# Two expert stages with short TensorE loop bodies, the bias added tile by tile, and 496 unrolled scatters

## The reference

```
h = gelu(einsum('td,edh->teh', xf, W1) + b1)      # 256 -> 512, every expert on every node
y = einsum('teh,ehd->ted', h, W2) + b2            # 512 -> 256
out = einsum('ted,te->td', y, gate)               # 8 experts, gate 0 or 1; then 4 experts, soft gate
```

## Time and profile before

| | |
|---|---|
| Median of three runs | 4744.22 us |
| Profiled execution, span | 5102.1 us |
| First expert stage, first POOL copy to first DVE instruction of the next stage | 1688.0 to 2725.6 us |
| PE in that stage, start of first and last matmul | 1694.2 and 2450.2 us |
| Second expert stage, the same of PE | 4718.8 and 5085.9 us |
| Busy: PE / DVE / ACT / POOL | 2674 / 1894 / 1149 / 2164 us |

### The profile page before, as it was taken

One profiled execution on the slowest core, in us unless ns is written; L12 is line 12 of the kernel. 1 busy time (PEld: TensorE's weight loads), 2 busy tenths in 40 slices (PEclk: granted clock), 3 DMA queues, 4 the chain that ended last, 5 costly groups with the idle time before them and its releaser, 6 DMA issues. The chain is left out here.

```text
span 5102.1 us, 58668 instructions
## 1 busy us (share of the span) xinstructions
PE 2674.1 (52%) x11127; PEld 1856.8 (36%) x11128; DVE 1893.5 (37%) x4714; ACT 1149.0 (23%) x3778; POOL 2164.1 (42%) x2734
## 2 busy tenths in 40 slices
PE   3223945665542399999203777774100001635898
PEld 2123923333321277777102333333100000423676
DVE  5600265656557711111002222223444445465411
ACT  0010022222210111111001111111466666310111
POOL 0165045555530665565562666660466665000000
PEclk8555556666655699999656666665555555555999
DMA  2111422222220000000001333330000000000000
GB/s 71 40 41 60 181 55 76 79 78 76 72 59 0 25 10 17 9 20 1 1 1 41 90 88 88 90 90 17 5 5 5 5 5 4 0 0 11 19 9 25
DMA packets 118123, 199.51 MB, mean 39 GB/s; under 512 B 54417, under 2 KB 81158, under 8 KB 115910
## 3 DMA queue, kind: packets, MB, share of 16 engines
q0 software_dynamic: 75360, 124.95, 10.1%
q1 hardware_dynamic: 42726, 74.12, 4.2%
HBM read 186.58 MB, written 12.36 MB: 39 GB/s over the span
## 5 line engine op out<-in xcount | busy, mean ns | idle before, releaser
L493 POOL DMA_INDIRECT a0rows<-table,a0idx x462 | 469.6, 1016 | 517.6 <-ACT a0idx L478 403.8
L493 POOL DMA_INDIRECT a1rows<-table,a1idx x444 | 421.5, 949 | 325.3 <-ACT a1idx L478 175.5
L950 POOL DMA_INDIRECT erecords<-sc_slot x416 | 408.5, 982 | 328.3 <-POOL sc_slot L946 311.7
L523 PE MATMUL a1ps<-a1rows,a1w 128*128 128x256 f32 x888 | 428.1, 605 | 191.9 <-DMA a1rows<-table,a1idx 135.3
L523 PE MATMUL a0ps<-a0rows,a0w 128*128 128x257 f32 x924 | 416.3, 585 | 177.0 <-DMA a0rows<-table,a0idx 82.7
L1146 POOL DMA_INDIRECT gt_land<-table_gat,gt_idx x324 | 356.8, 1101 | 249.9 <-POOL gt_idx L1141 162.2
L1341 ACT ACTIVATE gt_parts<-gt_nb,gt_land 128x128 f32 x1296 | 414.8, 392 | 20.7 <-DVE gt_parts L1191 1.8
L1363 PE MATMUL gt_psT<-k_ident,gt_top 128*128 128x128 f32 x100 | 27.9, 434 | 702.2 <-DVEq L1196 702.2
L749 PE MATMUL f0dn<-f0w,f0hid 128*128 128x256 f32 x1600 | 353.3, 380 | 61.9 <-DVE k_x L797 61.9
L523 PEld LDWEIGHTS a1ps<-a1rows,a1w 128*128 128x128 f32 x888 | 212.0, 279 | 408.1 <-issue 283.5
L764 PE MATMUL f0up<-k_xnT,f0w 128*128 128x320 f32 x1280 | 352.9, 435 | 12.8 <-DMA f0b<-in_f_b 12.8
(11 more groups left out here) (366 smaller groups left out, 4185.1 us busy)
## 6 DMA issues: line engine op xcount, KB each, us to landing
es_ea<-in_eaT SPq DMA_DIRECT2D x16, 1664.0 KB
es_lane<-lane_row SPq DMA_DIRECT2D x16, 832.0 KB
f0w<-in_f_W SPq DMA_DIRECT2D x16, 512.0 KB
a0rows<-table,a0idx POOLq DMA_INDIRECT x462
a1rows<-table,a1idx POOLq DMA_INDIRECT x444
erecords<-sc_slot POOLq DMA_INDIRECT x416
table<-k_tbl SPq DMA_DIRECT2D x10, 650.0 KB, 3.5
gt_land<-table_gat,gt_idx POOLq DMA_INDIRECT x324
```

The lines of the kernel that those rows point to most:

```text
L493: pool.indirect_dma_start(rows[:, i, 0:TW], None, table, bass.IndirectOffsetOnAxis(ap=idx[:, i:i + 1], axis=0)).then_inc(gathered[i], 16)
L523: nc.tensor.matmul(sum_of(t), w[:, i, :], rows[:, i, 0:width], start=False, stop=False).then_inc(agg_done, 1)
L950: pool.indirect_dma_start(self.rec_dram, bass.IndirectOffsetOnAxis(ap=slot[:, i, 0:1], axis=0), slot[:, i, 1:R + 1], None).then_inc(self.p ...
```

## The change

It has three parts, all in the functions around `emit_experts`, and nothing else of the kernel is touched.

1. **PE, ACT and DVE loops.** PE has an outer loop over expert pairs and in it two inner loops of 5 trips, one for each weight buffer. A trip is a step. The 640 columns of a step are now worked as 3 tiles and 2 tiles: 4 slices of 384 columns, then 4 slices of 256, then 3 down tiles and 2 down tiles. The outer loop is opened with an option that places its head at slot 0 of an instruction page. The up results use 2 PSUM banks of one slice each, the down results 5 banks, one per tile of a group. A down tile waits for the addition of the same tile in the step before. ACT has the same two-level loop and 8 Gelu instructions per step, of 384 and 256 columns, instead of 4 of 640.
2. **Bias.** DVE adds the bias for the 5 tiles of one step (L720 of the changed kernel), drains, and then adds the 5 down results of that step (L725).
3. **Scatters.** `DirectScatter` replaces `Scatter` for `sb` and `sc`: 496 indirect DMAs written out one after another with constant addresses, which read their records and their destination rows from the columns of `recg` and `rece` themselves. There is no copy, no wait on a copy and no register arithmetic. From the ninth on each waits for the transfer eight before it.

```diff
-    STEPS, HALF = 2 * OUT, U * P // 2
+    PER = 2 * KH
+    HALVES = ((0, 3), (3, U))
-        hid = [sb(f"hid{i}", [P, KH, 2, HALF], F32) for i in range(2)]
+        hid = [sb(f"hid{i}", [P, KH, (b - a) * P], F32) for i, (a, b) in enumerate(HALVES)]
-        up = [ctx.enter_context(nc.psum_tensor(f"{tag}up{i}", [P, 2, 512], F32)) for i in range(2)]
-        down = [ctx.enter_context(nc.psum_tensor(f"{tag}dn{i}", [P, 512], F32)) for i in range(4)]
+        up = [ctx.enter_context(nc.psum_tensor(f"{tag}up{i}", [P, 512], F32)) for i in range(2)]
+        down = [ctx.enter_context(nc.psum_tensor(f"{tag}dn{i}", [P, 512], F32)) for i in range(U)]
+        def add_tiles(v, e, g):
+            x_of = lambda j: S.x[:, bass.ds(g * (U * D) + j * D, D)]
+            gate_of = lambda j: gate[:, bass.ds(g * U + j, 1), bass.ds(e, 1)].rearrange("p a b -> p (a b)")
+            for j in range(U):
+                nc.vector.scalar_tensor_tensor(x_of(j), b2_rows[:, bass.ds(e, 1), :].rearrange("p a d -> p (a d)"), gate_of(j),
+                                               x_of(j), ALU.mult, ALU.add)
+            v.drain()
+            for j in range(U):
+                v.wait_ge(down_done, U + (e * OUT + g) * U + j + 1)
+                nc.vector.scalar_tensor_tensor(x_of(j), down[j][:, 0:D], gate_of(j), x_of(j), ALU.mult, ALU.add).then_inc(added, 1)
+            v.drain()
...
         def _(pe):
-            pe.sem_inc(down_done, 1)
-            with pe.Fori(0, n_experts // 2) as o:
-                def down_step(s):
...
-                for s in range(STEPS):
...
+            pe.sem_inc(down_done, U)
+            with nc.Fori(0, n_experts // 2, engines=[pe.engine], head_slot={pe.engine: 0}) as o:
+                for i in range(2):
+                    with pe.Fori(0, OUT) as g:
+                        turn = o * (2 * OUT) + (g + i * OUT)
+                        pe.wait_ge(arrived[i], o * 48 + 48)
+                        for half, (a, b) in enumerate(HALVES):
+                            size = (b - a) * P
+                            for m in range(KH):
+                                q = half * KH + m
+                                pe.wait_ge(hid_ready, turn * PER + q + 1)
+                                for k in range(KD):
+                                    ins = nc.tensor.matmul(up[q % 2][:, 0:size], w1[i][:, k, m * P:(m + 1) * P],
+                                                           S.xnT[:, k, bass.ds(g * (U * P) + a * P, size)],
+                                                           start=(k == 0), stop=(k == KD - 1))
+                                ins.then_inc(up_done, 1)
+                        for half, (a, b) in enumerate(HALVES):
+                            pe.wait_ge(hid_ready, turn * PER + (half + 1) * KH + 2)
+                            for j in range(a, b):
+                                pe.wait_ge(added, turn * U + j + 1)
+                                for k in range(KH):
+                                    ins = nc.tensor.matmul(down[j][:, 0:D], hid[half][:, k, (j - a) * P:(j - a + 1) * P],
+                                                           w2[i][:, k, :], start=(k == 0), stop=(k == KH - 1))
+                                ins.then_inc(down_done, 1)
...
         def _(v):
-            with v.Fori(0, n_experts) as e:
-                for t in range(NT):
-                    nc.vector.scalar_tensor_tensor(S.x[:, t * D:(t + 1) * D], b2_rows[:, bass.ds(e, 1), :].rearrange("p a d -> p (a d)"),
-                                                   gate[:, t, bass.ds(e, 1)], S.x[:, t * D:(t + 1) * D], ALU.mult, ALU.add)
-                v.drain()
...
+                with v.Fori(0, OUT) as g:
+                    add_tiles(v, e, g)
...
+class DirectScatter:
...
+    def run(self, pool):
+
+        R = self.rec.shape[2]
+        for c in range(self.first, self.last):
+            turn, lane = divmod(c - self.first, 8)
+            if turn:
+                pool.wait_ge(self.put[lane], 16 * turn)
+            pool.indirect_dma_start(self.rec_dram, bass.IndirectOffsetOnAxis(ap=self.rec[:, c + 1, 0:1], axis=0),
+                                    self.rec[:, c + 1, 1:R], None).then_inc(self.put[lane], 16)
...
-            beside = (Scatter(nc, S, "sb", recg, rec_dram, EARLY, GC, S.rec_sb, stage),
-                      Scatter(nc, S, "sc", rece, erec_dram, 0, NC, S.erec_sb, stage))
+            beside = (DirectScatter(nc, S, "sb", recg, rec_dram, EARLY, GC, S.rec_sb),
+                      DirectScatter(nc, S, "sc", rece, erec_dram, 0, NC, S.erec_sb))
```

More of the change, by code:

```diff
@@ L773, in _ @@
             nc.scalar.preload_act_table(ACT.Gelu)
-            act.sem_inc(hid_ready, 1)
+            act.sem_inc(hid_ready, 2)
             with act.Fori(0, n_experts // 2) as o:
[L776 to L781, removed]
+                for i in range(2):
+                    with act.Fori(0, OUT) as g:
+                        turn = o * (2 * OUT) + (g + i * OUT)
+                        for half, (a, b) in enumerate(HALVES):
+                            act.wait_ge(down_done, turn * U + b)
+                            for m in range(KH):
+                                q = half * KH + m
+                                act.wait_ge(up_done, turn * PER + q + 1)
+                                nc.scalar.activation(hid[half][:, m, :], up[q % 2][:, 0:(b - a) * P], ACT.Gelu,
+                                                     bias=bias1[i][:, m:m + 1]).then_inc(hid_ready, 1)
@@ L783, in _ @@
         @block.vector
         def _(v):
-            v.sem_inc(added, 1)
+            v.sem_inc(added, U)
             v.wait_ge(b2_in, 16)
             with v.Fori(0, n_experts) as e:
-                for t in range(NT):
-                    nc.vector.scalar_tensor_tensor(S.x[:, t * D:(t + 1) * D], b2_rows[:, bass.ds(e, 1), :].rearrange("p a d -> p (a d)"),
-                                                   gate[:, t, bass.ds(e, 1)], S.x[:, t * D:(t + 1) * D], ALU.mult, ALU.add)
-                v.drain()
@@ L792, in _ @@
[L792 to L799, removed]
-                    if s % OUT == OUT - 1:
-                        v.drain()
+                with v.Fori(0, OUT) as g:
+                    add_tiles(v, e, g)
@@ L936, in run_copied @@
                                         self.slot[:, i, 1:self.rec.shape[2]], None).then_inc(self.put[i], 16)
-    def run(self, pool):
-        nc, slot, R = self.nc, self.slot, self.rec.shape[2] - 1
-        def trip(o, is_first):
-            for i in range(8):
-                if not is_first:
-                    pool.wait_ge(self.put[i], 16 * (o - self.first))
-                count = pool.snap(o * 8 + (i + 1), min_val=1, max_val=self.last * 8)
-                nc.gpsimd.tensor_copy(slot[:, i:i + 1, :], self.rec[:, bass.ds(count, 1), :]).then_inc(self.copied, 1)
-                count = pool.snap(o * 8 + i + 1)
-                pool.wait_ge(self.copied, 1)
-                pool.wait_ge(self.copied, count)
-                pool.indirect_dma_start(self.rec_dram, bass.IndirectOffsetOnAxis(ap=slot[:, i, 0:1], axis=0),
-                                        slot[:, i, 1:R + 1], None).then_inc(self.put[i], 16)
-        if self.first:
-            pool.sem_inc(self.copied, self.first * 8)
-        with pool.Fori(self.first, self.first + 1) as o:
-            trip(o, True)
-        with pool.Fori(self.first + 1, self.last) as o:
-            trip(o, False)
     def finish(self, sp):
@@ L962, in finish, with __init__ @@
             sp.wait_ge(self.put[i], 16 * (self.last - self.first))
+        if self.rec_sb is not None:
+            sp.dma_start(self.rec_sb[:], self.rec_dram.rearrange("(p c) r -> p c r", p=P)).then_inc(self.back, 16)
+            sp.wait_ge(self.back, 16)
+class DirectScatter:
+    def __init__(self, nc, S, tag, rec, rec_dram, first, last, rec_sb=None):
+        self.nc, self.rec, self.rec_dram, self.rec_sb = nc, rec, rec_dram, rec_sb
+        self.first, self.last = first, last
+        self.back = S.sem(tag + "_back")
+        self.put = [S.sem(f"{tag}_put{i}") for i in range(8)]
+    def run(self, pool):
[6 more added lines that the diff above has]
+                                    self.rec[:, c + 1, 1:R], None).then_inc(self.put[lane], 16)
+    def finish(self, sp):
+        for i in range(8):
+            sp.wait_ge(self.put[i], 16 * ((self.last - self.first) // 8))
         if self.rec_sb is not None:
```

4 lines of the change are left out of this document (2 added, 2 removed).

## The result

The changed kernel takes 4398.19 us, the median of four runs (4397.0 to 4403.65), against 4745.63 us for the kernel before: a ratio of 0.927 with a 95% interval of 0.925 to 0.928, or 347 us less. The forecast was 4467 with a range of 4385 to 4625.

A forecast was written before the change was run, and what follows sets the result against it. POOL's scatters were taken to bound the first expert stage, PE after the change. That stage, 959 us with the surplus spread, falls to 703, gaining 256; with 20.6 from the second, 277 in all: 4467 us, range 4385 to 4625.

The forecast's parts named there:

- POOL's path: First expert stage: 496 scatters without copies at 1.27 or 1.28 us each, 634 us; bounds 486 us and the old 1.95 pitch.
- The bias rows against the scatters: First expert stage: DVE's bias rows, in runs of five, lengthen POOL's scatters by 51 us in all; bounds 0 and 94.
- the port decides: Rival, first expert stage: each run of five bias rows holds POOL throughout, POOL's path 737 against PE's 703; 4501 us, chance 0.07.
- PE, ACT and DVE: Both expert stages: steps stay 17.25 us, PE's wait for DVE goes; first stage 703 us, second gains 20.6.
- The wait of ACT between short slices: Expert steps: Gelu on 256-column slices expected covered; if not, up to 0.2 us per short slice, 48 us over 60 steps.
- a fetch on each trip: Rival, PE's expert loops: instructions fetched again each trip, 2.5 us for 60 trips gives 4617, 3.3 gives 4665; chance 0.08.
- The surplus of the first profiled execution: Span 357.9 us above the runs, spread evenly over all but the last stage (0.924): first expert stage 959 before, gain 256.
- a low clock: Rival, both expert stages: idle times between steps keep TensorE at 1.2 GHz, 34.5 us a step; 5500 us, slower, chance 0.03.

The follow-up runs named there:

- e6: Changed kernel with each of the 496 unrolled scatters preceded by the copy and a wait on it, as before, but with constants: 4440.52 us, ratio 0.936.
- e2: Kernel before with only the unrolled scatters of the change; its PE, ACT and DVE loops and the bias ahead stay: 4475.07 us, ratio 0.943.
- e5: Kernel before (old loops, four down banks) with the unrolled scatters and the bias added step by step: 4391.07 us, ratio 0.926.
- e10: e2 with DVE draining after every 5 bias rows instead of 25: 5388.31 us, beside 5098.23 for the kernel before.
- e1: Kernel before, unchanged, profiled once more: 4744.63 us, span 4742.8.
- e11: Changed kernel, unchanged, run again: 5370.86 us, ratio 1.053, beside 5098.23 for the kernel before.
- e4: Changed kernel with the bias added ahead for all experts and tiles, 25 instructions per trip, as before: 4484.34 us, ratio 0.944.
- e9: e5 with 40 scatters moved from the edge-score stage into the expert stage (EARLY 136): 5346.80 us, ratio 1.049, kernel before 5098.23.
- e12: Changed kernel with two transfers open instead of eight: 4398.69 us, ratio 0.927, beside 4749 for the kernel before.

## Why the prediction was right, and where it was not

- **POOL's path.** Sum: 634 us of scatters. Measured: 1385.4 to 2014.8 for the starts, 630. Right, and from the right row. The explanation, that the wait for the copy goes, was only a part: e6 gives 0.49 of 0.69 us to the loop. (1688.3 + 634 + 51 is 2373 and not 2374; nothing hangs on it.)
- **The bias rows against the scatters.** 51 us were taken, by the share of time in which DVE runs them, and about 4 measured (means of 963 and 968 ns against a median of 959). This term was mis-sized. What it should have been priced by is the length of one row without a gap: 10 us holds the third scatter up to 7.2 us, e2; 2.1 us holds none above 1.3, e5, the first 12 us of e10 and the changed kernel. The rival *the port decides* falls with it.
  The Trainium skill (SBUF — State Buffer, "SBUF: two separate sides") tells which instruction locks the port, and the traces agree: in the changed kernel scatters that meet L720 last up to 1.22 us and those that meet L725 alone at most 0.97, in e2 those beside L789 up to 7.22 and beside L797 at most 0.96. That scatters pass within the first 3 us of a row, in two rows the first 6, and in gaps of 0.17 us is what e2 and e10 add.
- **PE, ACT and DVE.** 17.25 per step forecast, 17.32 measured; up products of the first step dearer by 3.2 us instead of 2.2; the next stage starts 2.4 us behind PE's last matmul instead of 5. Stage 703 forecast, 705 measured. The second stage gives 19.4 instead of 20.6. The wait of ACT between short slices and a fetch on each trip did not appear: PE's matmuls have no idle time in 40 steps (its weight loads wait once per step for ACT, 0.2 us, behind a running matmul).
- **The surplus of the first profiled execution.** This is the step of the sum that failed. I spread 358 us evenly, and so took 78 us off the first expert stage that were never there; without it the sum is 4389, and 4398 was measured. e1 shows the stage at 1035 in an execution without surplus. The measured time lies 13 us above the lower end of the range, 4385, which was set next to this 4389. The mechanism was right and the centre was not; the range held because that end was left in it.
- **What the surplus was** is the true miss, since the row was there to be read. PE in the edge-score stage of the first trace of the kernel before:

```profile
269.85 0.18 PE L384 MATMUL es_ps<-es_parts,es_hot 128*128 128x25 bf16 x1 [2.63 <-issue]
272.64 0.18 PE L384 MATMUL es_ps<-es_parts,es_hot 128*128 128x25 bf16 x1 [2.61 <-issue]
...
278.24 1.58 PE L384 MATMUL es_ps<-es_parts,es_hot 128*128 128x25 bf16 x53 [2.60 <-issue]
...
481.44 0.18 PE L384 MATMUL es_ps<-es_parts,es_hot 128*128 128x25 bf16 x1 [2.65 <-issue]
...
485.65 1.18 PE L384 MATMUL es_ps<-es_parts,es_hot 128*128 128x25 bf16 x38 [0.51 <-issue]
```

  Stretches with one matmul each 2.8 us, and groups such as the 53 in 1.58 us between, until the last scatter of that stage has started (481.0), and five microseconds later full speed. The scatters beside it are 1.27 apart. In the first expert stage of that trace they are 1.95 apart, and PE was left alone. The change makes those 1.27 apart too. A rival "scatters at 1.27 starve PE in the expert stage as they do in the edge-score stage" would have come out of these rows, but not its price. At 2.8 us a matmul instruction 634 us of scatters make 226 of them, 3.1 steps of 72, and the other 36.9 at 17.25 follow: 1688 + 634 + 636 = 2958, so +232, and -20 in the last stage, slower by 212 us. With the groups counted the edge-score stage did 479 matmuls in the 238 us up to its last scatter, 0.50 us each; at that pace 17.7 steps are done beside the scatters, and the kernel is some 40 us faster. e11 measured 273 slower, at 2.80 us a matmul. The slower side of the prediction instead had a low clock, for 0.03. The granted clock is 0.53 in the window of e11, but PE is busy for 35 of its 200 us, so the idle time is what costs, and the clock is back at 1.00 when the steps follow each other again. The forecast of 0.96 for faster was too sure: kernels with these scatters came out faster on four occasions and slower on one.

What stays open: what the condition is. It was met in the first profiled execution and on one of the four occasions of the experiments, on the same chip that ran e1 to e4 without it some 19 minutes before. It was seen only beside indirect DMAs of POOL that are close together: the stages that grew in the first trace are those where they are mostly 1.25 to 1.3 apart, PE is untouched in the last stage, where POOL does nothing, and it isn't PE's loops (e9). The stage of 324 gathers with a copy each, mostly 1.95 apart (L1151 of the changed kernel), takes 723 us from first to last in e11 and 724 in the first trace of the same kernel. That the rate is the point, and not that the loops with copies do something else between, is argued from these two rates and was not tried in between.

## What to carry to other kernels

Before spreading a difference between a profiled execution and the runs over a kernel, look for rows that take longer than the same rows elsewhere in the trace; idle time of an engine on "issue", repeated at one step, names the place, and the change may extend exactly what runs beside it. Take a register loop around short POOL work apart by itself: constants gave more than leaving out the copy. And once the longest engine of a stage is relieved, price the wait of the next one: here PE's wait for DVE, hidden behind POOL in the first expert stage before, is worth 84 to 86 us once the scatters are fast (e2 against e5, e4).

## What the runs showed of the hardware

- An unrolled indirect DMA of 128 records costs POOL 0.96 us and 0.30 until the next, with eight transfers open. With two open it is the same in most places, but 16 of 496 wait for a transfer, 29 us in all (e12). In a register loop with a copy the period is 1.95, unrolled with the copy 1.46, unrolled without 1.27.
- DVE instructions with two SBUF inputs, 25 in a row, make one scatter of 0.96 us last up to 7.2 us; five in a row lengthen one by at most 0.3 (e2, e5).
- In one condition of the chip, a step of 72 matmuls takes PE 201.6 us instead of 17.3, with either form of its loops, as long as POOL scatters at 1.27 us (e9, e10, e11); DVE's instructions come 1.40 us apart in stretches (e10) and POOL's own scatters too (e11). Transfers are not slower. The cause isn't shown.
